# Expert routing in two batches of eight tiles instead of four batches of four, with the logits kept in one PSUM bank

## The reference

```python
x = x + xattn(layernorm(x), ctx, ctx, len, ...)      # out @ Wo + bo at its end
y = layernorm(x)
scores = einsum('td,ed->te', y, gate_w)              # 8 experts
weights, idx = top_k(softmax(scores), 2)
weights = weights / sum(weights)
x1 = silu(einsum('td,efd->tef', y, w1)); x3 = einsum('td,efd->tef', y, w3)
out_all = einsum('tef,edf->ted', x1 * x3, w2)
x = x + sum over the two chosen experts of weight * out_all[t, expert]
```

## Time and profile before

| what | value |
|---|---|
| median of the runs | 1263.69 us (1263.43 to 1264.68) |
| the profiled execution's own time | 1253.28 us |
| its span | 1251.5 us |
| mean granted clock of TensorE | 0.953 |
| busy, share of the span: PE, DVE, ACT, POOL | 87%, 79%, 58%, 52% |
| attention, to about | 934 us |
| projection and routing, about | 934 to 1047 us |
| expert tiles, about | 1047 to 1242 us |

### The profile page before, as it was taken

One profiled execution on the slowest core, in us unless ns is written; L12 is line 12 of the kernel. 1 busy time (PEld: TensorE's weight loads), 2 busy tenths in 40 slices (PEclk: granted clock), 3 DMA queues, 4 the chain that ended last, 5 costly groups with the idle time before them and its releaser, 6 DMA issues. The chain is left out here.

```text
span 1251.5 us, 33106 instructions
## 1 busy us (share of the span) xinstructions
PE 1089.7 (87%) x13006; PEld 712.1 (57%) x13006; DVE 983.8 (79%) x1793; ACT 730.1 (58%) x1297; POOL 654.4 (52%) x466
## 2 busy tenths in 40 slices
PE   1556999999999999999999999999959864999996
PEld 1322566556656656655665665666648752666663
DVE  5835899899899999889989999999935664555553
ACT  2522666666666666666666666666645552555553
POOL 1053674485476468458548646744449335323232
PEclk9667999999999999999999999999988886999999
DMA  8024232423433233242342333316636423333331
GB/s 271 1 69 101 78 90 54 110 79 85 102 84 99 63 104 91 53 116 76 82 110 84 91 76 93 84 41 217 214 103 219 136 85 94 56 50 54 54 55 15
DMA packets 103968, 117.03 MB, mean 94 GB/s; under 512 B 47293, under 2 KB 86014, under 8 KB 102526
## 3 DMA queue, kind: packets, MB, share of 16 engines
q1 hardware_dynamic: 91406, 100.46, 29.0%
q0 software_dynamic: 7152, 8.43, 3.9%
q10 hardware_dynamic: 5248, 5.92, 1.6%
HBM read 39.46 MB, written 36.87 MB: 61 GB/s over the span
## 5 line engine op out<-in xcount | busy, mean ns | idle before, releaser
L771 ACT ACTIVATE prob<-sc,key_bias 128x512 f32<-128x512 f32 x640 | 404.7, 683 | 149.4 <-PE sc L634 145.5
L852 DVE TENSOR_REDUCE part_max<-mx 128x1 f32<-128x427 f32 x768 | 418.1, 591 | 49.0 <-PE mx L646 49.0
L949 POOL TENSOR_TENSOR prob_lo<-prob 128x1024 bf16<-128x1024 f32 x128 | 242.2, 1892 | 239.5 <-ACT prob L771 239.2
L864 DVE TENSOR_TENSOR prob_lo<-prob 128x1024 bf16<-128x1024 f32 x192 | 276.0, 1438 | 10.6 <-ACT prob L771 7.0
L673 PE MATMUL pv<-VV,prob 128*128 128x65 bf16 x2560 | 267.9, 193 | 3.7 <-POOL prob_lo L949 3.5
L675 PE MATMUL pv<-VV,prob_lo 128*128 128x65 bf16 x2560 | 269.2, 195 | 0.0
L674 PE MATMUL pv<-VV,prob 128*128 128x64 bf16 x2560 | 267.9, 193 | 0.0
L673 PEld LDWEIGHTS pv<-VV,prob 128*128 128x128 bf16 x2560 | 239.7, 99 | 38.8 <-POOL prob_lo L949 7.3
L674 PEld LDWEIGHTS pv<-VV,prob 128*128 128x128 bf16 x2560 | 237.2, 97 | 26.4
L646 PE MATMUL mx<-K,Q 128*128 128x427 bf16 x768 | 237.2, 350 | 11.9 <-DMA K<-we 6.2
L633 PE MATMUL sc<-Q,K 128*128 128x512 bf16 x640 | 243.8, 381 | 1.1 <-ACT prob L771 1.1
(11 more groups left out here) (182 smaller groups left out, 1459.7 us busy)
## 6 DMA issues: line engine op xcount, KB each, us to landing
expert_inputs<-zeros SPq DMA_DIRECT2D x129, 129.0 KB, 2.6
Q<-we SPq DMA_DIRECT2D x48, 256.0 KB, 3.8
we<-in_w_exp SPq DMA_DIRECT2D x8, 1536.0 KB, 8.0
q32s<-q SPq DMA_DIRECT2D x128, 64.0 KB, 2.0
attention_out<-o_out SPq DMA_DIRECT2D x64, 128.0 KB, 1.9
o_in<-attention_out SPq DMA_DIRECT2D x16, 512.0 KB, 3.8
K<-we SPq DMA_DIRECT2D x48, 160.0 KB, 3.9
VV<-next_v SPq DMA_DIRECT2D x16, 322.5 KB, 4.1
```

The costliest lines, as they stand in the source:

```text
L771: act.activation(prob[:, s % PRING, j, :], sc[n % 2][:], ACT.Exp, bias=key_bias[:, t:t + 1], scale=HD ** -0.5).then_inc(exp_done, 1)
L852: dve.tensor_reduce(part_max[:, b_ % 2, qt, h:h + 1], mx[:, pl.part_banks(qt, h)[0]:pl.part_banks(qt, h)[-1] + 1, 0:pl.width], mybir.AxisL ...
L864: dve.tensor_tensor(prob_lo[:, s % PRING, 0:g, :], prob[:, s % PRING, 0:g, :], hi_half(prob[:, s % PRING, 0:g, :])[:, :, 1::2], ALU.subtra ...
L949: pool.tensor_tensor(prob_lo[:, s % PRING, 0:g, :], prob[:, s % PRING, 0:g, :], hi_half(prob[:, s % PRING, 0:g, :])[:, :, 1::2], ALU.subtr ...
```

## The change

There are now ROUTES = 2 batches of RT = 8 tiles. The first is chosen at the end of step 13, placed in step 14 and weighted in step 15 (its last tile has its logits in step 12); the second is routed behind the loop. All small tiles of the routing double in width. The logits of tile t go to their own eight columns of the bank `gp`, and DVE copies 64 of them at once at the head of `choose`; the only wait of PE's gate matmul for DVE that is left is at tile 8. The counts of `places` move to the upper half of bank `wp0`, where the projection of even tiles uses the lower, so there are waits on x1 and on `pc_read` around them; `counts` moves to `wp1`. On POOL the order is low 0, low 1, high 0, high 1: the separate `scatter_high(0)` between the lows is gone. PE waits for the end of POOL's weight split before the first expert tile.

```diff
+RT = 8
+ROUTES = ST // RT
...
-        g8 = [sb(f"g8_{i}", [P, QT, E]) for i in range(3)]
+        g8 = [sb(f"g8_{i}", [P, RT, E]) for i in range(3)]
...
-        pc = gp[:, E:E + ST * E]
-        counts = wp[0][:, 0:E]
+        pc = wp[0][:, D:D + ST * E]
+        counts = wp[1][:, 0:E]
...
@@ SP
-                for c in range(CH):
-                    sp.wait_ge(scattered_low[c], 16 * QT)
+                for c in range(ROUTES):
+                    sp.wait_ge(scattered_low[c], 16 * RT)
@@ ACT
-                    if step >= 2 * QT + 1 and (step - 1) % QT == 0:
-                        exponential((step - 1) // QT - 2)
-                exponential(CH - 1)
+                    if step == RT + 6:
+                        exponential(0)
+                exponential(1)
@@ POOL
-                    pool.tensor_tensor(half(we_lo, n), half(we, n), half(we_hi, n), ALU.subtract)
+                    pool.tensor_tensor(half(we_lo, n), half(we, n), half(we_hi, n), ALU.subtract).then_inc(we_split, 1)
                 pool.wait_ge(ids_made, 1)
                 scatter_low(0)
                 scatter_low(1)
-                scatter_high(0)
-                scatter_low(2)
-                scatter_low(3)
...
-                for c in range(1, CH):
-                    pool.wait_ge(scattered_low[c], 16 * QT)
+                for c in range(ROUTES):
+                    pool.wait_ge(scattered_low[c], 16 * RT)
@@ DVE, choose
-                    dve.wait_ge(gp_read, QT * (c + 1))
+                    dve.wait_ge(gp_ready, RT * (c + 1))
+                    dve.tensor_copy(left, gp[:, c * RT * E:(c + 1) * RT * E].rearrange("p (t e) -> p t e", e=E)).then_inc(gp_read, 1)
+                    dve.wait_ge(gp_read, c + 1)
@@ DVE, the steps
-                    if step >= 2 * QT + 1 and (step - 1) % QT == 0:
-                        place((step - 1) // QT - 2)
-                    if step >= 2 * QT + 2 and (step - 2) % QT == 0:
-                        weights((step - 2) // QT - 2)
-                    t = step - 5
-                    if 0 <= t < ST:
-                        dve.wait_ge(gp_ready, t + 1)
-                        dve.tensor_copy(logits[:, t, :], gp[:, 0:E]).then_inc(gp_read, 1)
-                    if step >= 2 * QT and step % QT == 0:
-                        choose(step // QT - 2)
-                place(CH - 1)
-                weights(CH - 1)
+                    if step == RT + 5:
+                        choose(0)
+                    if step == RT + 6:
+                        place(0)
+                    if step == RT + 7:
+                        weights(0)
+                choose(1)
+                place(1)
+                weights(1)
@@ PE
                     pe.wait_ge(chosen_made, c + 1)
-                    mine = pc[:, c * QT * E:(c + 1) * QT * E]
+                    if c > 0:
+                        pe.wait_ge(pc_read, c)
+                    mine = pc[:, c * RT * E:(c + 1) * RT * E]
...
+                        if t == RT + 6:
+                            pe.wait_ge(pc_read, 1)
...
-                    if step >= 2 * QT + 1 and (step - 1) % QT == 0:
-                        places((step - 1) // QT - 2)
+                    if step == RT + 6:
+                        pe.wait_ge(x1_made, RT + 5)
+                        places(0)
...
                             pe.wait_ge(gate_loaded, 16)
-                        else:
-                            pe.wait_ge(gp_read, t)
-                        if t >= QT and t % QT == 0:
-                            pe.wait_ge(pc_read, t // QT)
+                        if t == RT:
+                            pe.wait_ge(gp_read, 1)
                         for d in range(DT):
-                            ins = pe.matmul(gp[:, 0:E], YF[:, t % 2, d, :], gate_sb[:, d, :], start=d == 0, stop=d == DT - 1)
+                            ins = pe.matmul(gp[:, t * E:(t + 1) * E], YF[:, t % 2, d, :], gate_sb[:, d, :], start=d == 0, stop=d == DT - 1)
...
-                places(CH - 1)
-                pe.wait_ge(x1_made, ST - 1)
+                places(1)
+                pe.wait_ge(x1_made, ST)
...
                 first = pe.value_load(owner[0:1, 0:1], min_val=0, max_val=E - 1)
+                pe.wait_ge(we_split, 2 * E)
```

More of the change, by code:

```diff
@@ L1110, in experts @@
         logits = sb("logits", [P, ST, E])
-        g8 = [sb(f"g8_{i}", [P, QT, E]) for i in range(3)]
-        pick = [sb(f"pick{i}", [P, QT, E]) for i in range(2)]
-        top = sb("top", [P, 4, QT])
-        ew = sb("ew", [P, 4, QT])
+        g8 = [sb(f"g8_{i}", [P, RT, E]) for i in range(3)]
+        pick = [sb(f"pick{i}", [P, RT, E]) for i in range(2)]
+        top = sb("top", [P, 4, RT])
+        ew = sb("ew", [P, 4, RT])
         chosen = sb("chosen", [P, ST, E], BF16)
@@ L1135, in experts @@
         high_weighted, high_weights_set = sem("high_weighted"), sem("high_weights_set")
-        scattered_low, scattered_high = [sem(f"scattered_low{c}") for c in range(CH)], sem("scattered_high")
+        scattered_low, scattered_high = [sem(f"scattered_low{c}") for c in range(ROUTES)], sem("scattered_high")
         owner_made = sem("owner_made")
@@ L1374, in scatter_low @@
                     pool.wait_ge(low_weighted, c + 1)
-                    pool.wait_ge(nm_made, QT * (c + 1))
-                    for t in range(c * QT, (c + 1) * QT):
+                    pool.wait_ge(nm_made, RT * (c + 1))
+                    for t in range(c * RT, (c + 1) * RT):
                         pool.indirect_dma_start(x_slots, bass.IndirectOffsetOnAxis(slot[:, 0, t:t + 1], 0),
                                                 yrows[:, t, :], None).then_inc(scattered_low[c], 16)
-                def scatter_high(c):
-                    pool.wait_ge(scattered_low[c], 16 * QT)
[L1382 to L1386, removed]
-                                                yrows[:, t, :], None).then_inc(scattered_high, 16)
                 ids = yrows[:].bitcast(I32)
@@ L1409, in store @@
                                             bounds_check=S - 1, oob_is_err=False, compute_op=ALU.add).then_inc(y_stored[i % TURN], 16)
[L1411 to L1412 removed]
+                for c in range(ROUTES):
+                    pool.wait_ge(scattered_low[c], 16 * RT)
                     pool.wait_ge(high_weighted, c + 1)
[L1414 removed]
+                    some = slice(c * RT, (c + 1) * RT)
                     pool.tensor_copy(row_weights[:, some], high_weight[:, some]).then_inc(high_weights_set, 1)
                     pool.wait_ge(high_weights_set, c + 1)
[L1417 removed]
+                    for t in range(c * RT, (c + 1) * RT):
                         pool.indirect_dma_start(x_slots, bass.IndirectOffsetOnAxis(slot[:, 1, t:t + 1], 0),
@@ L1597, in places @@
                     pe.wait_ge(chosen_made, c + 1)
-                    mine = pc[:, c * QT * E:(c + 1) * QT * E]
+                    if c > 0:
+                        pe.wait_ge(pc_read, c)
+                    mine = pc[:, c * RT * E:(c + 1) * RT * E]
                     pe.matmul(mine, before_b[:], chosen[:, batch(c), :].rearrange("p t e -> p (t e)"), start=True, stop=False)
-                    for t in range(c * QT):
-                        pe.matmul(mine, ones_b[:], chosen[:, t:t + 1, :].to_broadcast([P, QT, E]), start=False, stop=False)
-                    for t in range(c * QT, (c + 1) * QT - 1):
-                        ins = pe.matmul(mine[:, (t + 1 - c * QT) * E:QT * E], ones_b[:],
-                                        chosen[:, t:t + 1, :].to_broadcast([P, (c + 1) * QT - 1 - t, E]),
-                                        start=False, stop=t == (c + 1) * QT - 2)
+                    for t in range(c * RT):
+                        pe.matmul(mine, ones_b[:], chosen[:, t:t + 1, :].to_broadcast([P, RT, E]), start=False, stop=False)
+                    for t in range(c * RT, (c + 1) * RT - 1):
+                        ins = pe.matmul(mine[:, (t + 1 - c * RT) * E:RT * E], ones_b[:],
+                                        chosen[:, t:t + 1, :].to_broadcast([P, (c + 1) * RT - 1 - t, E]),
+                                        start=False, stop=t == (c + 1) * RT - 2)
                     ins.then_inc(pc_ready, 1)
```

23 lines of the change are left out of this document (10 added, 13 removed).

## The result

| | before | changed |
|---|---|---|
| median of 11 runs each, same chip | 1264.68 us (1261.36 to 1267.18) | 1260.21 us (1256.18 to 1260.91) |
| profiled execution, its span | 1253.28, 1251.5 | 1260.7, 1258.9 |
| mean granted clock | 0.953 | 0.950 |

The ratio is 0.9954, 95% interval 0.994 to 0.9967: 4 to 8 us faster, where 6.4 were forecast. But the trace of the changed kernel is 7.4 us *longer* than the one of before. So the first thing to find out is whether the steps of the forecast are in it, and what else is.

The account below looks back on a forecast made before the run. No engine bounds the whole: PE, DVE with POOL, PE, then the stores in turn. Store 0 comes 6.1 us earlier through POOL, the last store 6.6; taking 6.4 from 1263.7 gives 1257.3 us, range 1254.6 to 1260.9.

Parts of the forecast that it names:

- start of step 14 earlier (5.15 + 2.73 + 1.74): PE's steps 9 to 13: without routing there, waits and slow-clock time vanish, so step 14 starts 9.62 us earlier.
- slack at the gate matmul and at the places: First routing, steps 13 to 15: PE has 0.2 us to spare at the gate matmul, 0.6 at the places; no cost.
- last OL late: DVE's last OL beside the first routing ends 9.15 us after step 14 starts, needed at 8.75: 0.4 late.
- step 14 to the last gate (T + 19.3): Tail of the projection: the last gate group ends 19.3 us after step 14 starts, bounds 17.5 and 21.3.
- last gate to first scatter: Last routing, twice as wide: 8.4 us to POOL's first scatter instead of 7.5.
- first low scatter to first expert matmul: Eight low scatters instead of four: PE's first expert matmul comes 19.6 us behind the first scatter, not 14.56.
- store 0 earlier, set by POOL: First store waits for POOL's last high scatter to land: 6.1 us earlier, at 1056.9, where PE alone allows 1054.7.
- first eight stores: After store 0, each store waits for the one ahead: 4.70 us each, 37.6 in all, bounds 36.8 to 38.8.
- The rule weighed: First routing's 3.18 us DVE comparison: by the GpSimd/VectorE SBUF contention rule, its new place is free of the hold.
- held in the first routing: DVE's 3 us stay or the gate matmul's 0.2 us slack is missed: gain 3.4 us, 1260.3; chance 0.16.
- The stores follow PE all the way: Stores at the end gain PE's 8.3 us: 1255.4, or 1253.6 with the short tail; chance 0.18.
- POOL's queue, slower: Eight more scatters, 10.2 us, before store 0; if step 9's loss moves to steps 13 to 15, 1266.2; chance 0.08.

Follow-up runs that it names:

- after_again: The changed kernel, unchanged, run again for a second trace; 1246.50 us.
- after_third: The changed kernel, unchanged, repeated on a chip where the kernel before took 1265.07; one run of 1255.25 us.
- after_timed: The changed kernel, unchanged, timed on another chip; 1249.01 against 1252.95 us for the kernel before, ratio 0.9952.
- quarters_late_lows_first: quarters_late with all low scatters ahead of all high ones on POOL; 1255.74 us, ratio 0.9927 to the kernel before.
- after_3high: The changed kernel with three high scatters of the first batch moved ahead of the second low batch; 1246.55 us, ratio 0.9943 to the kernel before.
- after_8high: The changed kernel without the eight high scatters of its first batch, leaving out part of the result; 1247.04 us.
- before_shift1: The kernel before with each routing one step later, still batches of four and POOL's old order; 1246.38 against 1253.75 us, ratio 0.995.
- quarters_late: The changed kernel with batches of four, place one step after choose, low and high scatters interleaved on POOL; 1243.89 us, ratio 0.9907 to the kernel before.

## Why the prediction was right, step by step

Against `after_again`, an undisturbed trace of the changed kernel, and the first trace of before:

| step of the prediction | forecast | measured |
|---|---|---|
| start of step 14 earlier (5.15 + 2.73 + 1.74) | 9.62 | 9.56 |
| slack at the gate matmul and at the places | no wait | no wait |
| last OL late | 0.4 | 0.17 |
| step 14 to the last gate (T + 19.3) | 19.3 | 18.95 |
| last gate to first scatter | 8.4 | 8.5 |
| last low scatter after the first | 8.9 | 8.92 |
| first low scatter to first expert matmul | 19.6 | 20.1 |
| first expert matmul earlier | 8.3 | 8.1 |
| first low to last high scatter | 29.6 | 29.8 |
| last high scatter to store 0 | 4.1 | 3.45 |
| store 0 earlier, set by POOL | 6.1 | 6.8, set by POOL |
| first eight stores | 37.6 | 38.6 |
| the end earlier | 6.4 | 6.3 |

Two terms were off and cancelled: the landing and what follows it took 0.65 less, the eight stores 1.0 more, within the bounds given (36.8 to 38.8). The gains by the ratios, 0.46% of 1264.68 and 0.48% of 1252.95, are 5.8 (4.2 to 7.6) and 6.0 (3.9 to 8.3) us, against 6.4; by the medians they are 4.5 and 3.9. The absolute forecast, 1257.3, is 2.9 below the median, a third of it because the kernel before itself came out 1.0 higher over 11 runs than over 3.

One sign that the prediction named did not come: after store 0 not every store waited for the one ahead. In `after_again` 25 did, the first 22 of them in a row, and 13 later ones were ACT's. It cost nothing, 141.4 us from store 8 to the last against 141.3.

**What was luck.** The prediction carried the 10.4 us between the profiled execution and the median over unchanged, without a reason. At the level of the first result both traces of the changed kernel (the first and `after_third`) have the pause, which puts their end at +320.8 and +319.0 instead of +310.8; that the kernel before loses about as much in its own median runs there is what the equal ratios suggest, and no trace shows it. The mechanism of the forecast is shown at the lower level, in `after_again` and `after_timed`; that its 6.4 us also fit the first result was not foreseen.

**The rule weighed.** The row was 3.18 us for a comparison that ended 0.05 after POOL's last subtraction. With the comparison 17 us behind (the changed kernel) or the subtractions held back it took 0.22 and 0.19; where it began 0.8 us ahead of the split's end (`quarters_late_lows_first`, 978.35, split until 979.13) it took 0.82. It ends with POOL's run, and that it is the first such instruction is nothing. This agrees with the Trainium skill, GPSIMD Engine Reference, Specifications, by which GpSimd's SBUF interfaces are shared with VectorE and instructions of VectorE with two SBUF inputs contend. The rival "held in the first routing" fell with it.

**The other rivals.** "The stores follow PE all the way" had the wrong owner of store 0 but was near: PE alone would have had store 0 1 to 2 us earlier (+120.8 in `after_3high`, +119.7 in `after_8high`). "POOL's queue, slower" needed the loss of step 9 to move into steps 13 to 15, and none of it did. In the first trace store 0 was released by ACT and came 3.8 us later than before, which the prediction names as a sign of being wrong; that was the pause, which no case had.

**Right in the sum, wrong in the weight.** The prediction booked 9.6 us of removed loss to the change as a whole; `before_shift1` shows that a delay of one step gives all of the gain, and the batches of eight with the logits in one bank next to none. Against it they bring the last gate matmul 7.2 us forward (+80.0 against +87.2, one routing fewer among the last steps), and then give it back: 0.9 between gate and scatter, 5.0 at the last low scatter, which starts 8.9 behind the first instead of 3.9, and 1.0 from there to the first expert matmul (11.1 against 10.2). The first expert matmul comes at +108.6 against +108.8. Then POOL has 24 scatters to send behind the last routing instead of 16, and store 0 is 0.7 later. `quarters_late` has an early last gate (+82.1) and the short last batch, and ends 5 to 6 us ahead of both. Its three differences from the changed kernel were not tried one by one; but `quarters_late_lows_first`, without its order on POOL, has the last gate at +81.2 and the first expert matmul at +104.7 all the same, so up to there the logits' own columns and the short batch bring it, not the order.

## What to carry to other kernels

Before two things are changed at once, ask what the smaller one does alone: here the delay by a step was the gain, and the batch size only a trade. Look at what runs beside an instruction that takes fifteen times its usual duration; moving either of the two removed the hold here and, with most of PE's wait, the slow step after it. A batch that stands at the end of a chain should be small, and work of a queue that can go out in an earlier idle time should not be left behind it.

## What the runs showed of the hardware

A pause of about 10 us. PE, DVE and ACT stand still (but for a few instructions in one trace) although what they wait for was done some 9 us earlier, and SP's small instructions take 0.7 us each; DVE is back 1.4 to 2.3 us after the last packet of POOL's scatters. It is in three of the five traces of kernels that send 16 high scatters behind the last low one, and in none of the nine others. That it goes with POOL's scatters in flight is what the three ends and SP's slow stretch in a fourth trace suggest; what brings it on in some executions and not in others is open.

It may also be part of what sets the two levels of the kernel before (1253 to 1256, and 1265); no trace of before caught it, so this is not shown. The changed kernel's 11 first runs lie in two groups as well, four up to 1257.35 and seven from 1259.65, but these the pause does not explain: it is in the trace of 1260.7 and in that of 1255.25, and 3.6 of the 5.5 us between them lie ahead of POOL's first instruction of the part (938.04 and 934.46). Since the ratio was 0.9954 at the one level and 0.9952 at the other, the level did not decide the result.

The other surprise is small. A comparison of DVE beside a run of POOL's subtractions looks stopped and not slowed: begun 3.1 us, twice 3.0 or 0.8 us ahead of the end of that run, it ended 0.04 to 0.06 us behind it. In the kernel before it was not let go where one subtraction ended (975.38) and the last began (975.34), but only behind the last (978.08). Other instructions of DVE beside the same subtractions were not held: OL, which has one input in PSUM, took 1.22 to 1.23 us as elsewhere.
